# Attention: SyncE reads u's turned rows back once the last projections of the turn are through

## The reference

```python
def step(carry, qkv):
    S_K, C_QV, G = carry
    q_t, k_t, v_t = qkv
    k_C = einsum('bhk,bhkv->bhv', k_t, C_QV)
    G = G + k_t[..., :, None] * k_C[..., None, :]
    S_K = S_K + k_t[..., :, None] * k_t[..., None, :]
    C_QV = C_QV + q_t[..., :, None] * v_t[..., None, :]
    S_C = einsum('bhkj,bhjv->bhkv', S_K, C_QV)
    o_t = einsum('bhk,bhkv->bhv', q_t, S_C - G)
    return (S_K, C_QV, G), o_t
```

## Time and profile before

| | us |
|---|---|
| median of 3 runs | 1029.08 |
| lowest and highest run | 1025.98, 1030.72 |
| the profiled execution's own time | 1030.74 |
| its span, first to last instruction | 1029.0 |
| PE busy in it | 1005.3 (98%) |
| DVE, ACT, POOL busy | 617.2, 491.0, 111.4 |
| granted clock of PE, mean | 0.998 of full speed |

### The profile page before, as it was taken

The page is one execution under the profiler, slowest core; times in us unless marked ns, Lnnn a source line. Parts: engine busy times, 40 slices in busy tenths (PEclk is TensorE's granted clock), DMA queues, the critical chain, the costliest instruction groups (busy, mean ns, idle before and its releaser), DMA issues.

```text
span 1029.0 us, 41963 instructions
## 1 busy us (share of the span) xinstructions
PE 1005.3 (98%) x19166; PEld 909.2 (88%) x19166; DVE 617.2 (60%) x1252; ACT 491.0 (48%) x925; POOL 111.4 (11%) x130
## 2 busy tenths in 40 slices
PE   8999999999999999999999999999999999999998
PEld 7788798999998998899999999988899888889887
DVE  7888877763445545555465465553564457767773
ACT  5676766643343433333443344333443344456663
POOL 2461331220000000000000000000000000113130
PEclk9999999999999999999999999999999999999999
DMA  9422000023324233242242333332333333200101
GB/s 314 154 59 82 1 2 1 1 83 115 115 85 131 90 95 126 69 143 85 96 136 90 101 124 101 111 101 69 126 106 106 104 126 94 97 22 21 42 31 52
DMA packets 60735, 92.75 MB, mean 90 GB/s; under 512 B 7056, under 2 KB 50448, under 8 KB 59536
## 3 DMA queue, kind: packets, MB, share of 16 engines
q1 hardware_dynamic: 60288, 90.07, 26.6%
q10 hardware_dynamic: 272, 0.00, 0.0%
HBM read 48.63 MB, written 41.42 MB: 88 GB/s over the span
## 4 chain that ended last, share of the span: by engine, by line
PE 95%; ACT 2%; issue 1%; DVE 1%; POOL 0%; POOLq 0%; ACTq 0%; DVEq 0%
PE bank L223 7%; PE bank L224 6%; PE bank L1185 6%; PE bank L225 6%; PE bank L1211 6%; PE bank L1196 5%; PE bank L1245 4%; PE bank L1233 3%; PE bank L1175 3%; PE bank L1222 3%; PE bank L805 3%; PE bank L807 3%; PE bank L1246 3%; PE bank L1247 3%; PE bank L1261 3%; PE bank L1177 3%
## 5 line engine op out<-in xcount | busy, mean ns | idle before, releaser
L1471 ACT COPY qt<-bank 128x512 f32<-128x512 f32 x64 | 37.6, 587 | 157.0 <-PE bank L225 157.0
L1607 DVE STREAM_TRANSPOSE k<-kt 128x512 f32<-128x512 f32 x64 | 43.4, 697 | 106.6 <-ACT kt L1466 55.6
L1466 ACT COPY kt<-bank 128x512 f32<-128x512 f32 x64 | 37.5, 587 | 114.5 <-PE bank L225 114.5
L1628 DVE TENSOR_TENSOR state_s<-bank,state_s 128x256 f32<-128x256 f32 x124 | 46.8, 420 | 74.5 <-ACT ut L1484 72.5
L223 PE MATMUL bank<-ln_xhi,wk_hi 128*128 128x256 f32 x256 | 75.9, 296 | 0.0
L223 PE MATMUL bank<-ln_xhi,wq_hi 128*128 128x256 f32 x256 | 75.4, 294 | 0.0
L1245 PE MATMUL bank<-wo_hi,ot_hi 128*128 128x256 f32 x256 | 75.0, 293 | 0.0
L1518 ACT ACTIVATE D_hidden<-bank,b_sb 128x512 f32<-128x512 f32 x64 | 44.1, 690 | 59.6 <-PE bank L1262 59.6
L224 PE MATMUL bank<-ln_xlo,wk_hi 128*128 128x256 f32 x256 | 72.5, 283 | 0.0
L224 PE MATMUL bank<-ln_xlo,wq_hi 128*128 128x256 f32 x256 | 72.3, 283 | 0.0
L225 PE MATMUL bank<-ln_xhi,wk_lo 128*128 128x256 f32 x256 | 72.3, 282 | 0.0
(11 more groups left out here) (161 smaller groups left out, 2904.9 us busy)
## 6 DMA issues: line engine op xcount, KB each, us to landing
k_rows_scratch<-k SPq DMA_DIRECT2D x32, 512.0 KB, 2.7
k<-k_rows_scratch SPq DMA_DIRECT2D x128, 128.0 KB, 2.9
u_rows_scratch<-sc_and_k SPq DMA_DIRECT2D x31, 512.0 KB, 3.4
landed<-u_rows_scratch SPq DMA_DIRECT2D x124, 128.0 KB, 3.0
out_dram<-xres SPq DMA_DIRECT2D x16, 256.0 KB, 2.1
xres<-in_L_attn_a_x_dram SPq DMA_DIRECT2D x7, 512.0 KB, 10.5
w_nat<-in_L_ffn_W_dram SPq DMA_DIRECT2D x2, 1024.0 KB, 9.8
raw<-in_L_attn_b_W_q_dram SPq DMA_DIRECT2D x1, 1024.0 KB, 12.9
```

## The change

Before the four reads of u's rows are issued in turn `j`, SP now waits for one thing more. In an odd turn it is the second half of that turn's `values`, in an even turn the last quarter of the block of q. Turn 30, which has no such block, gets no wait. Nothing else changes on any engine.

```diff
                 def land_u(j):
                     if j:
                         sp.wait_ge(urow_done, 2 * j)
+
+                    if j % 2:
+                        sp.wait_ge(v_ready, 2 * (j + 1))
+                    elif q_block(j):
+                        sp.wait_ge(q_ready, 4 * (q_block(j) + 1))
                     land_rows(rows_dram["u"], landed, u_saved, u_landed, j)
```

## The result

The changed kernel takes 1024.28 us (median of 6 runs, 1023.75 to 1025.07) against 1029.34 of the kernel before in the same comparison (6 runs, 1025.98 to 1030.72): ratio 0.9958, 95% interval 0.9942 to 0.9974. It is 5.1 us faster where 1.5 was forecast. The profiled execution has a span of 1022.8 us, 6.2 less than that of before. All lines of the kernel behind the change have moved by 5: L1185 is L1190, L1196 is L1201, L1200 is L1205, L1233 is L1238.

What follows compares the result with a forecast made beforehand. The prediction took PE to bound the kernel, with 8.3 us of "issue" idle time in attention. A gain of 1.5 us, all other terms at 0, gave 1029.2 us profiled, 1027.6 against the median; range 1023.5 to 1033.5.

Steps and rivals of the forecast that it cites:

- What bounds the kernel: PE, busy 1005.3 of 1029.0 us; only its idle time can move the end, 8.3 us of "issue" in attention.
- what the idle times are: PE's "issue" waits in attention are instruction fetches that come too late at packet borders, such as 2.00 us in turn 23.
- Where the reads start: Reads of u's rows move some 2.6 us later in even turns, 1.2 in turn 13, nearly nothing else.
- who waits for them: ScalarE copies u's rows 8 us after they land in turn 12, 5 us or more in other moved turns: 0 us.
- what is queued behind: On SP behind the wait: the next save of k comes 5 to 10 us later, w1's load moves 2 us: 0 us.
- What is won: Starts of turns 9 and 23 idle 1.10 us each instead of 1.69 and 2.00: 1.5 us won, at most 3.7.
- the load of w1: Behind turn 28's reads, moved by 2 us: valued at 0, with 0.6 us less and 2 more as ends.
- What may be lost: Reads of other even turns now overlap the next turn's first fetch: loss about nothing, upper bound the slower rival.
- the slower rival: Reads hold the fetch after every even turn, new idle 4 to 6 us into odd turns: 1039 us; chance 0.08.
- Rival 1: Reads don't matter to the fetch, which is late anyway; nothing visible changes: 1029.1 us; chance 0.20.
- Rival 2: All idle time at starts behind even turns goes, and turn 29's 0.61 us: 4.3 us, 1024.8; chance 0.09.
- Within 0.5%: 0.81: Chance of no difference, between 1023.9 and 1034.2 us; faster got 0.09 and slower 0.10.

Runs made afterwards that it cites:

- the paddings: Changed kernel with 16, 48 or 64 redundant waits added on PE ahead of turn 0: 1023.13, 1026.61 and 1021.79 us.
- the second pair of traces: The kernel before and the changed kernel, both unchanged, traced once more: 1029.67 and 1025.46 us in one execution each.
- the even turns alone: Against the kernel before, only even turns wait before the reads of u's rows: 1025.40 us, ratio 0.9965.
- a quarter of the traffic: Kernel before, without the new wait; from turn 1 each read of u's rows fetches only its first quarter: 1025.16 us, ratio 0.9964.
- the later placing: Changed kernel, but every turn's reads wait until the next turn's scores are through, some 2 us later: 1030.37 us, ratio 1.0005 to the kernel before.
- the two with 48 waits: 48 redundant waits added on PE ahead of turn 0: 1031.74 us in the kernel before, 1026.61 us in the changed one.
- the wait in odd turns alone: Against the kernel before, only odd turns wait before the reads of u's rows: 1029.11 us, ratio 0.9995.

## Why the prediction was right or wrong

Its direction and range held (1023.5 to 1033.5), and so did its mechanism for the starts of turns; its sum was a third of what was measured, since it put two other gains at nothing.

- *What bounds the kernel; what the idle times are.* Right on the idle times, and shown by the paddings; what it left out is PE's busy time, below.
- *Where the reads start; who waits for them; what is queued behind.* Right to 0.2 us: even turns at 0.14 us after the turn's start, ACT's copies and the saves of k unmoved. No new wait of PE for the copies came up.
- *What is won.* I took 1.10 us for both starts, from one odd turn. They measured 0.86 and 0.92, which gives 1.9 us instead of 1.5; the second pair of traces gives 1.1. So this term was about right. All waits before L1185 came to 2.6 us and not to the 4.2 that I had named, but 0.96 of the difference is turn 28, which I can't credit to the change. The larger omission lies behind the idle time. The prediction starts from "only what lengthens or shortens PE's idle time can move the end", and this step failed, as the busy time fell by 2.8 us too: the kernel before runs at half clock for 3.4 us after the 2.00 us of turn 23, 1.5 us more. I had read the row at 711.00 and stopped there. The next rows (0.41 us where the same line takes 0.28) and the mean clock of 0.998 in my own table were the sign. In the 71 timed runs of the kernel before that came with the experiments, the mean granted clock was 0.9976 on average, and 22 of them had 0.999 or more. All 6 of the changed kernel had that, all 6 of the even turns alone and all 6 with a quarter of the traffic. Of 1029 us, 0.0024 are up to 2.5 us. The 22 runs have a median of 1027.8 us and the other 49 one of 1029.9, 2.1 more; over all 71 runs that is about 1.4 us by this count. The clock is likely a good part of the 3.6 us missing in my sum, and some of it is counted again in the load of w1 below. That it follows from the idle times is argued from four traces, not shown in each run.
- *The load of w1.* Valued at 0 with 0.6 as the gain's end; this is the other term that was mis-sized, as it is worth 1.5 to 2 us. I took one trace's 0.61 us for the size. The next trace has 2.26, with a half-clock stretch behind it.
- *What may be lost.* The 1.21 us in turn 3 (0.99 in the second trace, 0.00 and 0.40 in those of before) are of the slower rival's kind, once instead of twelve times, and not at its place (7 us into the turn, not 4 to 6). The rival's rule, that a fetch is held until the reads are drained, fits the later placing better than this one.
- *Rival 1* is refuted by the quarter of the traffic, which won 3.7 us (by the ratio) at the old place: the traffic ahead does cost the fetch time. The Trainium skill's rule behind this rival (DMA: Bandwidth & Descriptors, "Queues, rings and completion order"; a fetch would wait for one packet) gave the wrong time here, and the measurement decides. The Trainium skill's other page (Runtime: NRT & Kernel Launch, "Instruction fetch mechanics") agrees with the traces on blocks of 256 instructions; its "mostly hidden" holds for most of the 151 fetches, but those that aren't cost 5 to 8 us in the four traces of the two kernels.
- *Rival 2* had the nearest time, 1024.8 us against 1024.28, but not for its reason. The starts of turns 9 and 23 still wait 0.86 and 0.92 us, where it had nothing. It was right on turn 29.
- *Within 0.5%: 0.81.* 0.42% lies within it, but the interval reaches to 0.58%. The forecast of 0.15% made this look safer than it was, and that the measured time stayed above 1023.9 us, by 0.4, is in part luck.

## What to carry to other kernels

When PE is 98% busy and its rest is "issue" before groups of small matmuls, count the instructions between these places: if they are multiples of one number, look at which DMA traffic lies ahead of the instruction fetches there, and move it to where wide matmuls follow. Read also the rows behind a long idle time, for durations at half clock, before pricing it. Place bulk loads by the same rule as the small reads, and time a few paddings of PE's stream before you trust a difference of half a per cent: the borders alone moved the changed kernel by 4.8 us.

## What the runs showed of the hardware

PE's instructions came in blocks of 256 (one of 16.4 KB for each 254 matmuls and weight loads). Its idle times for "issue" in the turns stood only at borders between blocks, and there mostly where it had worked for less than some 3 us since the last one, though not at each of these. From the start of a fetch to PE going on it was 2.2 to 3.0 us at every idle time of the turns, in all traces. Data traffic of 512 KB ahead of a fetch held it by 0.7 us at the start of turn 23, and by 0.3 at that of turn 9.

I hadn't expected that idle times of some 2 us on PE would be followed by 3.4 us at 1.2 GHz. Both traces of before show it, behind 2.00 and 2.26 us. So do the two with 48 waits, behind 1.94 us in the kernel before and, 1.5 us after PE went on, behind 1.73 us in the changed one, so the change as such doesn't prevent it. This is the window of the latter, which starts 0.5 us ahead of the fall and so has 0.58:

```profile
282.90:286.30 3.40, 3.40 (x20) 3.40 (x19) 0.00 (x0) 0.59 (x1) 0.00 (x0) 0.58 0.32 90
```

It doesn't always follow. The trace with the wait in odd turns alone has 1.96 us idle in turn 9, 2.26 in turn 29 and a granted clock of 1.0 throughout the turns.
